# Three-step graph network: the order of groups from a stagger of three to groups in fours, with a prologue for four first layers

## The reference

```python
def L0(x): return einsum('nm,bmd->bnd', adj, x) @ weight + bias
x = layernorm(x + L0(x))                       # first layer
h = x
for _ in range(3):                             # three gated steps
    a  = einsum('nm,bmd->bnd', adj, h)
    av = concatenate([a, a], axis=-1)
    z  = sigmoid(av @ w3.T + h @ u3.T + biases)
    r  = sigmoid(av @ w4.T + h @ u3.T + biases)
    hv = tanh(av @ w5.T + (r * h) @ u5.T + biases)
    h  = (1 - z) * h + z * hv
out = layernorm(x + h)
```

## Time and profile before

| what | us |
|---|---|
| median of 3 runs | 1696.18 |
| the profiled execution, its own time | 1698.56 |
| its span, first to last instruction | 1696.7 |
| PE busy in the span | 1614.2 |
| DVE, ACT, POOL busy | 1450.4, 946.3, 246.0 |
| mean granted TensorE clock | 0.974 |

### The profile page before, as it was taken

The page is one execution under the profiler, slowest core; times in us unless marked ns, Lnnn a source line. Parts: engine busy times, 40 slices in busy tenths (PEclk is TensorE's granted clock), DMA queues, the critical chain, the costliest instruction groups (busy, mean ns, idle before and its releaser), DMA issues.

```text
span 1696.7 us, 21577 instructions
## 1 busy us (share of the span) xinstructions
PE 1614.2 (95%) x7616; PEld 1355.4 (80%) x7616; DVE 1450.4 (85%) x1902; ACT 946.3 (56%) x1353; POOL 246.0 (15%) x295
## 2 busy tenths in 40 slices
PE   5689999999999999999999999999999999999883
PEld 4578888888888888888888888888888888888662
DVE  4577899988999998899989899998989999898763
ACT  2345566656566655655665565566556566656432
POOL 1001111111111111111111111111111111110001
PEclk7799999999999999999999999999999999999987
DMA  4244454555555455555545555554555555445331
GB/s 147 87 137 155 143 186 159 159 164 178 182 178 172 156 170 163 173 186 169 175 156 171 159 177 186 165 166 166 167 162 180 186 162 173 159 158 180 126 121 63
DMA packets 198012, 272.45 MB, mean 161 GB/s; under 512 B 19216, under 2 KB 169232, under 8 KB 197904
## 3 DMA queue, kind: packets, MB, share of 16 engines
q1 hardware_dynamic: 197904, 271.07, 50.2%
HBM read 136.78 MB, written 134.22 MB: 160 GB/s over the span
## 4 chain that ended last, share of the span: by engine, by line
PE 92%; DVE 3%; DMA 2%; SPq 1%; ACT 1%; issue 1%; POOL 0%; ACTq 0%; POOLq 0%; DVEq 0%
PE ps_r L274 46%; PE ps_h L274 30%; PE ps_a L310 8%; PE ps_l L296 5%; PE ps_l L286 3%; DMA a_scratch_b<-a_blocks_b 0%; DMA a_scratch_a<-a_blocks_a 0%; DMA bias_in<-biases 0%; DVE hv L587 0%; DMA a_landed_a<-a_scratch_a 0%; DMA a_landed_b<-a_scratch_b 0%; DVE hv L584 0%; SPq L193 0%; DVE nat_lo L501 0%; DVE a_blocks_b L549 0%
## 5 line engine op out<-in xcount | busy, mean ns | idle before, releaser
L446 ACT ACTIVATE rh<-ps_r,bias_r 128x512 f32<-128x512 f32 x192 | 132.4, 690 | 153.4 <-PE ps_r L274 153.4
L384 ACT ACTIVATE rh_hi<-rh 128x512 fp32r<-128x512 f32 x192 | 119.2, 632 | 104.9 <-DVE rh L574 104.4
L464 ACT ACTIVATE hv<-ps_h,bias_h 128x512 f32<-128x512 f32 x192 | 130.9, 687 | 69.4 <-PE ps_h L274 69.0
L501 DVE TENSOR_TENSOR rh_lo<-rh,rh_hi 128x512 fp32r<-128x512 f32 x192 | 126.5, 690 | 9.2
L668 POOL TENSOR_TENSOR out_var_eps_sb<-out_meanvar,eps 128x4 f32<-128x4 f32 x32 | 7.6, 238 | 849.0 <-DVE out_meanvar L512 849.0
L587 DVE TENSOR_TENSOR hv<-hv,z_sb 128x1024 f32<-128x1024 f32 x96 | 117.7, 1226 | 10.0
L274 PE MATMUL ps_r<-a_hi_b,w_hi 128*128 128x512 f32 x384 | 120.5, 395 | 4.2 <-ACT a_hi_b L384 4.2
L460 ACT ACTIVATE z_sb<-ps_r,bias_z 128x512 f32<-128x512 f32 x192 | 120.4, 673 | 4.7 <-PE ps_r L274 4.5
L274 PE MATMUL ps_r<-h_hi,u_hi 128*128 128x512 f32 x384 | 121.1, 397 | 1.3 <-ACT z_sb L460 1.3
L274 PE MATMUL ps_r<-h_lo,u_hi 128*128 128x512 f32 x384 | 120.3, 395 | 0.8 <-DVE h_lo L501 0.8
L274 PE MATMUL ps_r<-h_hi,u_lo 128*128 128x512 f32 x384 | 120.7, 396 | 0.0
(11 more groups left out here) (177 smaller groups left out, 4056.3 us busy)
## 6 DMA issues: line engine op xcount, KB each, us to landing
a_scratch_a<-a_blocks_a SPq DMA_DIRECT2D x48, 512.0 KB, 2.6
a_landed_a<-a_scratch_a SPq DMA_DIRECT2D x192, 128.0 KB, 3.0
h_scratch_a<-h_blocks_a SPq DMA_DIRECT2D x48, 512.0 KB, 4.3
h_landed_a<-h_scratch_a SPq DMA_DIRECT2D x192, 128.0 KB, 2.9
a_scratch_b<-a_blocks_b SPq DMA_DIRECT2D x48, 512.0 KB, 2.6
a_landed_b<-a_scratch_b SPq DMA_DIRECT2D x192, 128.0 KB, 2.9
h_scratch_b<-h_blocks_b SPq DMA_DIRECT2D x48, 512.0 KB, 4.2
h_landed_b<-h_scratch_b SPq DMA_DIRECT2D x192, 128.0 KB, 2.8
```

The costliest lines, as they stand in the source:

```text
L384: return act.activation(dst, src, ACT.Copy)
L446: act.activation(rh[:, c, :], ps_r[:, c, :], ACT.Sigmoid, bias=bias_r[:, c:c + 1]).then_inc(r_ready, 1)
L464: act.activation(hv[:, c, :], ps_h[:, c, :], ACT.Tanh, bias=bias_h[:, c:c + 1]).then_inc(hv_ready, 1)
L501: return dve.tensor_tensor(dst, full, hi.bitcast(F32), ALU.subtract)
```

## The change

**The order.** Groups run in fours: step 0 of four groups in four slots, then step 1 of the four, then step 2, then the next four. All 96 slots are full. First layers of groups 4 and up run every third slot from slot 0. The last state of a group is moved, summed and stored later, by two slots more for each place in its four, except for the last four groups.

```diff
-    def slot_of(g, t):
-        return 3 * g + 4 * t
+    FOUR = 4
+    ROUND = FOUR * STEPS
+    def slot_of(g, t):
+        return ROUND * (g // FOUR) + FOUR * t + g % FOUR
+    def output_slot(g):
+        return slot_of(g, STEPS - 1) + 1 + (0 if g >= GROUPS - FOUR else 2 * (g % FOUR))
-    GRAPH, WEIGHTS, NORM = -6, -4, -3
-    SUM_UP, RESULT = 2 + 8, 3 + 8
+    GRAPH, WEIGHTS, NORM = -12, -10, -9
+    SUM_UP, RESULT, STORE = 1, 2, 3
```

```diff
+            pe.wait_ge(idle_ready, 1)
+            for _ in range(10):
+                pe.matmul(ps_r[:, 0, 0:P], idle_in[:, :], idle_in[:, :], start=True, stop=True)
+            pe.wait_ge(adj_in, 16)
+            first_graph(0)
+            first_graph(1)
+            pe.wait_ge(w0_ready, 1)
+            first_weights(0)
+            first_graph(2)
+            first_weights(1)
+            first_weights(2)
+            first_graph(3)
+            graph(0)
+            first_weights(3)
+            a_products(0)
+            graph(1)
+            pe.wait_ge(gates_ready, 3)
+            state_product(0)
+            first_layer(0)
+            gates(0)
+            for s in range(1, SLOTS):
...
+            def graph_by_features(g):
+                pe.wait_ge(h0_ready, g + 1)
...
+                rows = in_batches(h0_nat[FOUR + g])
+                for c in range(C):
+                    for b in range(G):
+                        mm = pe.matmul(ps_a[:, c, :].rearrange("p (j b e) -> p j b e", b=G, e=Q)[:, :, b, :],
+                                       rows[:, b, c * P:(c + 1) * P], adjt[:, :].rearrange("p (j e) -> p j e", e=Q),
+                                       start=True, stop=True)
+                mm.then_inc(a_done, 1)
```

**SP's loop.** A slot can now hold two moves of a state:

```diff
-                if s - 1 in nth:
-                    move_h(s - 1)
+                if 1 <= s <= SLOTS and at(s - 1)[1] < STEPS - 1:
+                    move_h(nth_move[at(s - 1)])
+                for g in output_at(s, 0):
+                    move_h(nth_move[g, STEPS - 1])
```

More of the change, by code:

```diff
@@ L174, in weights, with load_gate, load @@
                 return w.rearrange("(c p) o -> p c o", p=P)
[L176 to L185, removed]
+            def load_gate(name, w):
+                sp.dma_start(w_raw[name] if name in w_raw else u_raw[name], weights(w)).then_inc(gate_in[name], 16)
+            def load(g):
+                if g >= X_RING:
+                    sp.wait_ge(h0_ready, g - X_RING + 1)
+                sp.dma_start(x_in[g % X_RING][:, :, :], x_groups[g]).then_inc(x_loaded[g % X_RING], 16)
             def to_dram(dst, blocks, written):
@@ L243, in store @@
                 sp.dma_start(out_groups[g], result[g % 2][:, :, :]).then_inc(out_stored[g % 2], 16)
-            for s in range(BEGIN, END + 5):
-                h0_next = group_at(s, NORM + 1)
+            sp.dma_start(adjt[:, :], adj_t).then_inc(adj_in, 16)
+            load(0)
+            sp.dma_start(w0_raw[:, :, :], weights(w0)).then_inc(w0_in, 16)
+            sp.dma_start(bias_row[:, :], b0.to_broadcast([P, D])).then_inc(bias_in_s, 16)
+            load(1)
+            load(2)
+            load_gate("w4", w4_t)
+            load(3)
+            load_gate("w5", w5_t)
+            load_gate("u3", u3_t)
+            load_gate("w3", w3_t)
+            load_gate("u5", u5_t)
+            sp.dma_start(bias_in[:, :, :], biases).then_inc(gate_bias_in, 16)
+            write_h0(0)
+            read_h0(0)
+            load(4)
+            for s in range(END + 1):
+                h0_next = group_at(s, NORM + 1) if s + 1 >= FOUR else s + 1
                 if h0_next is not None:
                     write_h0(h0_next)
-                if s + 1 in nth:
+                if FOUR <= s + 1 < SLOTS:
                     write_a(s + 1)
@@ L606, in _ @@
             low_part(w0_lo[:, :, :], w0_raw[:, :, :], w0_hi[:, :, :]).then_inc(w0_ready, 1)
-            for s in range(BEGIN, END + 5):
-                if s + 1 in nth:
+            first_graph_low(0)
+            first_graph_low(1)
+            first_sum(0)
+            gate_halves("w4")
+            first_graph_low(2)
+            first_sum(1)
+            gate_low("w4")
+            gate_halves("w5")
+            first_blocks(0)
+            first_graph_low(3)
+            graph_low(0)
+            first_sum(2)
```

485 lines of the change are left out of this document (294 added, 191 removed).

## The result

The changed kernel takes 1642.75 us, the median of 4 runs (1641.22 to 1646.79), beside 1696.72 us for the kernel before in the same session: a ratio of 0.9686, interval 0.9666 to 0.9705. It is 54 us faster. The forecast was 1635.4 us with a range of 1625 to 1652: right in direction, inside the range, 7 us too low. The profiled execution took 1646.79 us, with a span of 1645.0 and a mean granted clock of 0.990.

The account below looks back on a forecast made before the run. PE was taken as the bound, 95% busy, with losses at both thin ends. Span: 1696.7 - 27.2 (end) - 39.5 (start) + 1.9 (more work) + 4 (doubles) = 1635.9, so median 1635.4 us; range 1625 to 1652.

Parts of the forecast that it names:

- The end: After 1601.33 us: full slots to the 96th regain all 27.2 us lost; 23.3 us behind the last product stay.
- The start: Before slot 2: PE's loss falls from 59.6 to 20.1 us, a gain of 39.5; slot 2 starts at 73.4.
- The zeros: Idle products before 5.5 us: end near 3 us, gain 0 to 1.7 us, taken as 0.
- The table load: On ACT before the first sigmoid: priced at its row's 1.28 us; the skill's drain would add 1.4.
- The middle: Full slots: PE's order stays; the only new cost is second state moves on SP, +4 us.
- double: A slot where SP moves two states: twelve, each 0 to 1.0 us, taken as 0.35, +4 in all.
- rival 1: Middle: doubles cost 1 to 2.2 us each, as the second move's traffic slows a's landing; about 1650 us, chance 0.22.
- tail: After PE's last product: stays 23 us; 0 to 1.5 us more if store 29 slows the last move.
- Rival 2: Start does not fill: one late link on SP or ACT raises the loss from 20 to 35; 1650 us, chance 0.14.
- rival 3: Start and middle: idle products keep the clock up, loss 15, doubles free; 1626 us, chance 0.07.
- Rival 4: Middle: SP falls behind for good after doubles, needing 5.4 us each; 1700 us, chance 0.05 shared with Rival 5.
- Rival 5: Middle: the stagger's cover filled it, so four neighbours at one step collide; chance 0.05 shared with Rival 4.

Follow-up runs that it names:

- e8: The changed kernel with paired moves (the paired kernel): in a double slot SP issues both writes, then both reads; 1633.8 us.
- e12: The kernel of e8 without the ten products of zeros at the start and the wait for their input; 1633.69 us.
- e11: The kernel of e8 with the first layers of groups 0 to 3 all in one bank pair and one pair of rounded halves; 1645.94 us.
- e0: The changed kernel itself, measured again as the base for other runs on its chip; 1646.84 us.
- e3: The changed kernel with the outputs' extra delay removed, so no slot holds two state moves; 1661.3 us.
- e5: The changed kernel with u5 and w3 rounded ahead of slot 1's a_hi and a_lo and group 3's sum; 1646.99 us.
- e6: The changed kernel with group 1's rows (x_in_b) loaded ahead of w0 and the bias row; 1645.16 us.
- e4: The changed kernel with ACT making z ahead of a_hi in slots after a double move; 1644.31 us.

## Why the prediction was right, and where it was off

**The end**: right. The forecast took all 27.2 us; PE is full to its last product at 1621.64, and 23.4 us follow (23.3 forecast).

**The start**: right in shape, 2.7 us short. The chain by hand put x_in_b at 10.7 (11.09), weight product 2 at 22.5 (23.64), graph of group 4 to 44.9 (it starts at 44.93), the wait for the first sigmoid at 5.6 (5.69) until 50.5 (52.65), slot 2 at 73.4 (76.13). The loss is 76.1 - 53.3 = 22.8 us, not 20.1. Of the 2.7, 1.1 are there at 18.59: the low clock was charged once for graph 1, and the rows show it on graph 1 and on the weight product after it (14.53 to 18.59). Another 0.7 come before the graph product of group 4 (44.93 for 43.1), 0.3 before the sigmoid, and 0.6 in slot 0 behind it (8.1 us from w3 to the end for 7.5). In e8, where graph 1 took 2.05, slot 2 started at 72.70. The zeros end at 5.6, not 3: ten fp32 products are 20 records, twice my estimate. The same holds for what I called 16 matmuls of a first layer's graph product: the code issues 8, and the 16 are records. That did not matter for the sum, since its prices are those of whole groups, and e12 shows the zeros worth nothing. The spread over banks, which the forecast used without pricing it, is worth 12.1 us (e11).

**The table load**: its row's 1.28 was the right price. The Trainium skill (ScalarE: Activation LUTs, What ACT_TABLE_LOAD costs) adds 1.38 of drain; here slot 2 moved by 1.33 when the load went, so by this measurement there is no drain to pay at that place.

**The middle** is the weak step, by size. "I take 0.35 x 12 = +4" was 9.7 us in the profile shown, 0.8 for each double in place of 0.35, inside the 0 to 1.0 that I had worked out and below rival 1's 1 to 2.2. The mechanism is the one forecast, link by link (SP's second move, read of a, a_hi, z, PE), and it stood "only one slot after a double move, ended by z_sb". The term that I mis-sized is the slip of the read of a. I had SP free 1.3 to 3.1 us after its h0 write of today and carried 1.1 to 2.6 of that to the read; the rows show 3.1 in the mean of twelve (2.0 to 4.2). I took the low end because the second move would run while the queue is quiet, but from its write to its read passed 3.84 us in the mean of 14 (3.49 to 5.38), in the upper half of the 2.6 to 4.4 that I gave it, and once outside. That the cost stayed at 0.8 is in part luck: a landed 5.4 us after its issue in the mean, where my one row before had 6.4. e8 shows the cause by removing it: the excess fell from 10.3 to 0.1. I also counted twelve doubles of fourteen and put the last two, behind which no first layer runs, at nothing; slots 89 to 93 lost 0.8 us (1.3 in e0), and none in the paired kernel.

**The account** for the span, 1645.0 against 1635.9: start +2.7, doubles +5.7, slots 89 to 93 +0.8, tail +0.1, 9.3 of 9.1. For the median it goes otherwise. Each execution here lasts 1.8 us longer than its span, while the forecast set the median 0.5 below a span, that of a slower execution; so of the 7.35 us that the median lies over 1635.4, 2.3 come from that step, and some 5 from the losses. The start and the doubles both came out above their terms, and the range had room for both.

**The rivals.** Rival 1 is the forecast's own mechanism at a higher price, and the price lies between the two; its reason does not hold, since a lands no later after its issue behind a double (5.4 us) than without one (5.6). Rival 2 (loss 35) did not come; rival 3 neither, e12 speaks against it. Rival 4 needed 5.4 us per double; the slot after a stalled one shows 0.2 of excess at most, so the delay does not build up. Rival 5 did not show in the paired kernel: with the moves paired, four neighbours at one step leave PE full. e3 showed a rival that I had not named here: with outputs undelayed DVE is full, and rh, a_hi, two norms and z on ACT come late behind it.

## What to carry to other kernels

An engine that issues a transfer, waits for it to land and only then issues the next one pays each landing in series; issue all the writes that are ready first, then wait. Here that was one loop of SP split in two, and it was worth 13 us, the two edits at the start 5.3. Judge an edit at the start on a base whose middle does not stall, since e5 and e6 gained 4 to 5 us there and showed none in the total until the stalls were gone. When a late input blocks an in-order engine, moving its neighbour ahead (e4) may only pass the loss to another pair of engines; shortening what makes it late holds.

## What the hardware did that I had not expected

A DVE tensor-tensor of 1024 columns with both inputs in SBUF that starts while POOL runs one ends 1.08 to 1.09 us after POOL's end: 3.46 us for 1.22, seven times in e4 and six in e3, and 2.15 for 1.18 on nat_lo. With one input in PSUM (nat_lo from ps_l at 15.97 in the change, inside POOL's 14.96 to 17.34) it keeps its 1.22, and a block transpose beside the same POOL instruction its 1.25. The Trainium skill (SBUF — State Buffer, Terms) calls the port pair of the two engines exclusive, "held for the full instruction"; the rows agree where both inputs lie in SBUF.

Taking one Sigmoid on a tile of 16 bytes into the kernel made about a quarter of the gates', state and graph products up to 8 ns longer, 7.4 us in all, with the granted clock unchanged; all later tiles had moved by 32 bytes. And the same start code gave 3.78, 3.28 or 2.05 us for the same 16 products, so a low-clock price read from one profile has an error of about 1.7 us.
